# Router scores and ranks: from two TensorE products with the identity to a trip through memory, and the choice of kept tokens one step later

## What is computed

```python
scores = jnp.einsum('bld,d->bl', x, w_r) + b_r
_, idx = jax.lax.top_k(scores, k)
x_sel = jnp.take_along_axis(x, idx[:, :, None], axis=1)
h = jax.nn.gelu(jnp.einsum('bkd,df->bkf', x_sel, w1) + b1)
out_sel = jnp.einsum('bkf,fd->bkd', h, w2) + b2
out = jnp.zeros_like(x).at[batch_ix, idx].set(out_sel)
```

## Time and profile before

| | |
|---|---|
| median of 3 runs | 1942.69 us (1942.07 to 1943.33) |
| profiled execution, its own time | 1942.34 us |
| its span, first to last instruction | 1940.5 us |
| mean granted TensorE clock | 0.986 |
| PE, DVE, ACT, POOL busy | 95%, 75%, 65%, 65% of the span |
| router's first and last product with the identity | start at 1005.4 us and 1857.8 us |

### The profile page before, as it was taken

One profiled execution on the slowest core, in us unless ns is written; L12 is line 12 of the kernel. 1 busy time (PEld: TensorE's weight loads), 2 busy tenths in 40 slices (PEclk: granted clock), 3 DMA queues, 4 the chain that ended last, 5 costly groups with the idle time before them and its releaser, 6 DMA issues.

```text
span 1940.5 us, 30226 instructions
## 1 busy us (share of the span) xinstructions
PE 1837.5 (95%) x9439; PEld 1281.6 (66%) x9439; DVE 1456.8 (75%) x2572; ACT 1260.5 (65%) x3937; POOL 1265.2 (65%) x1252
## 2 busy tenths in 40 slices
PE   6889999999999999988599899999999999999998
PEld 6667777777777777655255575756657575665765
DVE  8889999999999999997555565655656565565522
ACT  5778888888888888865355574655646465564621
POOL 4779999999999999988676545444544544450000
PEclk9999999999999999999699999999999999999999
DMA  5333223332333323320767334434343343431021
GB/s 203 128 127 143 110 112 138 144 132 100 127 144 144 133 95 132 131 87 29 209 203 206 112 89 111 120 108 122 93 139 99 109 119 108 119 94 59 29 66 39
DMA packets 133198, 228.59 MB, mean 118 GB/s; under 512 B 31076, under 2 KB 86388, under 8 KB 128048
## 3 DMA queue, kind: packets, MB, share of 16 engines
q1 hardware_dynamic: 99952, 161.38, 23.9%
q0 software_dynamic: 33088, 65.28, 12.0%
HBM read 209.99 MB, written 44.70 MB: 131 GB/s over the span
## 4 chain that ended last, share of the span: by engine, by line
PE 46%; ACT 2%; issue 1%; DMA 1%; DVE 1%; POOL 0%; DVEq 0%; SPq 0%; ACTq 0%; POOLq 0%
PE attn_psum L1909 12%; PE attn_psum L1925 11%; PE attn_psum L1828 5%; PE attn_psum L1841 5%; PE attn_psum L1821 4%; PE attn_psum L1867 3%; PE attn_psum L1812 2%; PE attn_psum L1943 2%; PE attn_psum L1802 1%; PE attn_psum L1853 1%; ACT xh L1554 1%; ACT th L1555 1%; DMA kv_at<-kv_scratch,new_now 0%; ACT prob L1512 0%; ACT k_t L1502 0%
## 5 line engine op out<-in xcount | busy, mean ns | idle before, releaser
L996 DVE TENSOR_TENSOR_SCAN hid<-scan_psum,dbu 128x1024 f32<-128x1024 f32 x256 | 593.8, 2320 | 10.6 <-ACT scan_psum L635 10.6
L1161 PE MATMUL scan_psum<-hid,ident 128*128 128x256 f32 x2048 | 519.0, 384 | 24.1 <-POOL hid L492 23.8
L1161 PEld LDWEIGHTS scan_psum<-hid,ident 128*128 128x128 f32 x2048 | 378.8, 191 | 185.7 <-issue 106.5
L1663 DVE CUSTOM_DVE_ANT_0 prob<-attn_psum,mask 128x336 f32<-128x336 f32 x256 | 120.1, 505 | 287.2 <-PE attn_psum L1821 287.0
L492 POOL TENSOR_TENSOR hid<-hid,kv_at 128x1024 f32<-128x1024 f32 x128 | 306.5, 2407 | 29.8 <-DVE hid L996 29.4
L492 POOL TENSOR_TENSOR hid<-hid,bc 128x1024 f32<-128x1024 f32 x128 | 305.8, 2401 | 28.6 <-DVE hid L996 28.2
L1518 ACT COPY p_t<-attn_psum 112x384 f32<-112x384 f32 x256 | 122.3, 484 | 291.5 <-PE attn_psum L1828 291.5
L1925 PE MATMUL attn_psum<-w,ffn_hid 128*128 128x512 f32 x512 | 239.0, 596 | 4.9 <-DVE y_sb L1728 4.9
L1446 POOL DMA_INDIRECT kv_at<-kv_scratch,new_now x189 | 200.4, 1060 | 61.6 <-issue 57.0
L1909 PE MATMUL attn_psum<-xs_in,w 128*128 128x256 f32 x1024 | 232.6, 381 | 7.5 <-ACT xs_in L1524 6.6
L635 ACT ACTIVATE scan_psum<-delta,neg_a 128x252 f32<-128x252 f32 x512 | 211.3, 464 | 10.6 <-DVE hid L996 10.6
(11 more groups left out here) (222 smaller groups left out, 3047.7 us busy)
## 6 DMA issues: line engine op xcount, KB each, us to landing
bc<-bc_scratch SPq DMA_DIRECT2D x16, 2048.0 KB, 7.4
kv_at<-bc_scratch SPq DMA_DIRECT2D x15, 2048.0 KB, 7.3
q_scratch<-qg SPq DMA_DIRECT2D x32, 260.0 KB, 2.0
early<-q_scratch SPq DMA_DIRECT2D x32, 260.0 KB, 3.0
x_pair<-in_x_pairs SPq DMA_DIRECT2D x32, 256.0 KB, 2.7
kv_scratch<-kvg SPq DMA_DIRECT2D x32, 256.0 KB, 2.0
a_scratch<-a_sb SPq DMA_DIRECT2D x32, 256.0 KB, 3.2
w_o<-x_scratch SPq DMA_DIRECT2D x32, 256.0 KB, 3.2
```

The lines of the kernel that those rows point to most:

```text
L996: nc.vector.tensor_tensor_scan(hid[:, k % RING, :, :].rearrange("p n t -> p (n t)"), decay[k % 2], dbu[:, k % RING, :, :].rearrange("p n t ...
L1161: mm = nc.tensor.matmul(yc, ident[:], hid[:, k % RING, i, :], start=False, stop=(k % 4 == 3 and i == 3))
```

## The change

The two products with the identity are gone. `r_s` is stored to a scratch row in memory (`store_scores`) and loaded back as the whole row on every partition (`load_scores`, into `s_row`); `r_rank` goes the same way into 64 partitions of `rank_row`. VectorE compares with `r_s` itself, so the product that gave `r_own` goes too. `router_keep` moves from window 1 to window 2. `turn_o` waits for the copy of the previous output out of the bank instead of for the previous selection. In pairs 31 to 33 some of the work sits at other windows, since windows 2 and 3 are short or empty there. The fill of `ones` and TensorE's wait for it go.

```diff
@@ SyncE
+            def store_scores(m):
+                sp.wait_ge(dve_s, m + 1)
+                sp.dma_start(S["score"][m], r_s[:]).then_inc(st_s, 16)
+            def load_scores(m):
+                sp.wait_ge(st_s, 16 * (m + 1))
+                wait(sp, dve_rank, m)
+                sp.dma_start(s_row[:], S["score"][m:m + 1].rearrange("m p o -> (m p o)").partition_broadcast(P)
+                             ).then_inc(ld_s, 16)
+            def store_ranks(m):
+                sp.wait_ge(dve_rank, m + 1)
+                sp.dma_start(S["rank"][m], r_rank[:]).then_inc(st_rank, 16)
+            def load_ranks(m):
+                rows = slice(64 * (m % 2), 64 * (m % 2) + 64)
+                sp.wait_ge(st_rank, 16 * (m + 1))
+                wait(sp, dve_keep, 2 * m)
+                sp.dma_start(rank_row[rows, :], S["rank"][m:m + 1].rearrange("m p o -> (m p o)").partition_broadcast(64)
+                             ).then_inc(ld_rank, 16)
...
                 if parts.prev2:
+                    store_ranks(m - 2)
+                    load_ranks(m - 2)
                     store_keep(m - 2, 2 * i + j // 2 - 1, h)
...
+                if parts.prev:
+                    store_scores(m - 1)
                 if parts.second and j in (1, 2):
                     store_out(i - 2, j - 1)
+                if parts.prev:
+                    load_scores(m - 1)
@@ GpSimd
-            nc.gpsimd.memset(ones[:], 1.0).then_inc(filled, 1)
@@ ScalarE
-                    if w == 2 and parts.prev:
+                    if w == (2 if parts.own else 1) and parts.prev:
                         take_a(m - 1, 2 * i + j // 2, 1 - h)
@@ VectorE
             def router_rank(m):
-                row = a_bank[:, 0:P]
-                dve.wait_ge(pe_row, m + 1)
-                v.tensor_tensor_reduce(r_junk[:, 0:P], row, ident[:], 1.0, 0.0, ALU.mult, ALU.add, r_own[:]
-                                       ).then_inc(dve_rc, 1)
-                dve.wait_ge(dve_rc, 4 * m + 2)
-                v.scalar_tensor_tensor(r_junk[:, P:2 * P], row, r_own[:], own[:], ALU.is_gt, ALU.mult,
+                dve.wait_ge(ld_s, 16 * (m + 1))
+                dve.wait_ge(dve_s, m + 1)
+                v.scalar_tensor_tensor(r_junk[:, P:2 * P], s_row[:], r_s[:], own[:], ALU.is_gt, ALU.mult,
                                        accum_out=r_gt[:]).then_inc(dve_rc, 1)
...
             def router_keep(m, i, j):
-                dve.wait_ge(pe_rank, m + 1)
+                dve.wait_ge(ld_rank, 16 * (m + 1))
...
-                        if w == 3:
+                        if w == (3 if parts.own else 1):
                             router_score(m - 1)
                     if parts.prev2:
                         if w == 0:
                             router_rank(m - 2)
-                        if w == 1:
+                        if w == (2 if parts.nxt else 1):
                             router_keep(m - 2, i if j > 1 else i - 1, (j - 2) % 4)
@@ TensorE
             def turn_o(m):
                 pe.wait_ge(act_o, m + 1)
-                wait(pe, dve_keep, 2 * m)
+                wait(pe, act_a, m)
...
-            def router_row(m):
-                pe.wait_ge(act_a, m + 1)
-                pe.wait_ge(dve_s, m + 1)
-                nc.tensor.transpose(a_bank[:, 0:P], r_s[:].to_broadcast([P, P]), ident[:]).then_inc(pe_row, 1)
-            def router_ranks(m):
-                pe.wait_ge(dve_rank, m + 1)
-                nc.tensor.transpose(a_bank[:, P:2 * P], r_rank[:].to_broadcast([P, P]), ident[:]).then_inc(pe_rank, 1)
...
-                    if w == 2 and parts.prev:
+                    if w == (2 if parts.own else 1) and parts.prev:
                         turn_o(m - 1)
...
-            pe.wait_ge(filled, 1)
```

More of the change, by code:

```diff
@@ L1205, in attention_ffn_block @@
         ident = W["ident"]
-        ones = sb("ones", [P, P])
         w_o = sb("w_o", [P, 4, D])
@@ L1240, in attention_ffn_block @@
         r_idx = [sb(f"r_idx{i}", [P, 1], I32) for i in range(2)]
-        r_own, r_gt, r_eq, r_rank = (sb(n, [P, 1]) for n in ("r_own", "r_gt", "r_eq", "r_rank"))
+        r_gt, r_eq, r_rank = (sb(n, [P, 1]) for n in ("r_gt", "r_eq", "r_rank"))
+        s_row, rank_row = sb("s_row", [P, P]), sb("rank_row", [P, P])
         keep_t = [sb(f"keep_t{i}", [P, P]) for i in range(2)]
@@ L1676, in router_score @@
                 dve.wait_ge(act_a, m + 1)
[L1677 removed]
+                wait(dve, st_s, 16 * m)
+                wait(dve, dve_rank, m)
                 v.tensor_tensor_reduce(r_junk[:], a_sb[:], w_or[:], 1.0, 0.0, ALU.mult, ALU.add, r_s[:]
                                        ).then_inc(dve_rc, 1)
[L1680 removed]
+                dve.wait_ge(dve_rc, 3 * m + 1)
                 v.tensor_tensor(r_s[:], r_s[:], b_r[:], ALU.add).then_inc(dve_s, 1)
             def router_rank(m):
[L1685 to L1690 removed]
+                dve.wait_ge(ld_s, 16 * (m + 1))
+                dve.wait_ge(dve_s, m + 1)
+                v.scalar_tensor_tensor(r_junk[:, P:2 * P], s_row[:], r_s[:], own[:], ALU.is_gt, ALU.mult,
                                        accum_out=r_gt[:]).then_inc(dve_rc, 1)
[L1692 removed]
+                v.scalar_tensor_tensor(r_junk[:, 2 * P:3 * P], s_row[:], r_s[:], before[:], ALU.is_equal, ALU.mult,
                                        accum_out=r_eq[:]).then_inc(dve_rc, 1)
[L1694 removed]
+                dve.wait_ge(dve_rc, 3 * m + 3)
+                wait(dve, st_rank, 16 * m)
                 v.tensor_tensor(r_rank[:], r_gt[:], r_eq[:], ALU.add).then_inc(dve_rank, 1)
@@ L1700, in router_keep @@
                 rows = slice(64 * h, 64 * h + 64)
-                dve.wait_ge(pe_rank, m + 1)
+                dve.wait_ge(ld_rank, 16 * (m + 1))
                 wait(dve, st_keep[h], 16 * (2 * i + j // 2))
-                v.scalar_tensor_tensor(keep_t[h][rows, :], a_bank[rows, P:2 * P], slot_no[rows, :], slot_own[rows, :],
+                v.scalar_tensor_tensor(keep_t[h][rows, :], rank_row[rows, :], slot_no[rows, :], slot_own[rows, :],
                                        ALU.is_equal, ALU.mult).then_inc(dve_keep, 1)
@@ L1957, in pair @@
                         turn_x(i - 1, j - 1)
-                    if w == 0 and parts.prev2:
-                        router_row(m - 2)
-                    if w == 1 and parts.prev2:
-                        router_ranks(m - 2)
                     if w < 2 and parts.own:
@@ L2010, in program @@
     S["wid"] = nc.dram_tensor("wid_scratch", [NWC, P], F32).ap()
+    S["score"] = nc.dram_tensor("score_scratch", [NG, P, 1], F32).ap()
+    S["rank"] = nc.dram_tensor("rank_scratch", [NG, P, 1], F32).ap()
     S["keep"] = nc.dram_tensor("keep_scratch", [NG, 2 * SEL, P], F32).ap()
```

9 lines of the change are left out of this document (3 added, 6 removed).

## The result

The changed kernel takes 2062.05 us (median of 6 runs, 2055.58 to 2069.25), the kernel before 1942.38 (6 runs, 1941.41 to 1943.33): 1.0617 of it, 95% interval 1.0594 to 1.0639. The forecast was 1939.4 us, with a chance of 0.12 for slower. The profiled execution has a span of 2059.7 us, 119.2 more than before.

The account below looks back on a forecast made before the run. TensorE was taken to bound the second phase; 3.9 us saved on products less 0.6 us lost in pairs 2 to 4 gave -3.3 us, so 1939.0 on the profiled execution and 1939.4 as median, range 1935.5 to 1945.

Parts of the forecast that it names:

- The scores' trip, steady: Pairs 7 to 30: store and load back take 5.4 us, inside a gap of 5.8 to 7.7; cost 0.
- the sign of its being wrong: The prediction is wrong if a round trip through memory takes over 9 us; one of three such signs.
- The rival on the other side: Scores' trip slow in every pair, 4-byte pieces being slower; at 10 us a trip 1958 us; chance 0.12, above 1946.6.
- The cover, 9.2 us: Steady pairs: 5.8 us gap plus 3.4 us slack; a scores' trip costs TensorE time only above 9.2 us.
- What leaves TensorE, 6.8 us: 64 products, two for each of 32 pairs, at 0.106 us each: at most 6.8 us saved.
- what is absorbed: 27 of 64 removed products stand ahead of TensorE stops and buy nothing; 37 remain, 3.9 us saved, bounds 3.5 and 6.8.
- the three stops: TensorE's waits for `xs_in`, `y_sb` and at `turn_k`, on average 0.8, 0.7 and 0.36 us, grow by 0.1 each.
- Pairs 2 to 4, 0.6 us (0 to 4): Ranks' store queues behind weight loads, VectorE stands 8 us at `router_keep`, `norms` barely on time; 0.6 us lost, bounds 0 and 4.
- The tail, 0 us (at most 2): Last pairs: the last gather lands at 1867 or 1868.6, ahead of TensorE's need at 1870.82; cost 0, upper bound 2 us.
- The ranks' trip, 0: Steady pairs: the ranks' trip has a whole window more, 13 us or so; cost 0.
- VectorE's added work: L1687 goes, about 0.3 us a pair, and compares read SBUF; VectorE is not the bound, so 0.
- the start: Removing the fill of `ones` at 948.97 saves 0 to 0.2 us; taken as 0.

Follow-up runs that it names:

- x9: Repeat of the changed kernel with scores and ranks turned by VectorE's 32x32 transpose, stored as four pieces of 128 bytes: 1936.71 us, 0.9975 of the kernel before.
- x1: The changed kernel, but VectorE turns scores and ranks first, so each store is four pieces of 128 bytes: 1937.33 us, 0.9976 of the kernel before.
- x2: The kernel before with the changed kernel's four transfers a pair added and read by nobody; rows and ranks still come by products: 1944.4 us, 1.0013.
- x10: The changed kernel with the scores' 4-byte store kept, the ranks' store turned and the compare in window 1: 1962.57 us, 1.0104 of the kernel before.
- x13: The changed kernel with turned stores and three added scores' stores, each waited for, in a disturbed time: 1.0205 of the kernel before.
- x17: Turned stores with three added scores' stores again, in another disturbed call: 1.0263 of the kernel before.
- x12: The changed kernel with turned stores and the scores stored twice, one after the other has landed: 1936.35 us, 0.9971 of the kernel before.
- x4: The kernel before with only the ranks sent through memory and tokens chosen in window 2; scores by the product: 1950.93 us, 1.0043.

## Why the prediction was wrong, step by step

**The step that failed** is in "The scores' trip, steady": "The nearest are the store of `keep_t`, 2.1 us to landing ... 2.1 + 3.2 + 0.1 = 5.4 us, just inside." The store took 7.2 us and the load 4.2 to 4.9, so the trip was 11.4 us in the pair shown and 12.7 in the median. That is above the 9 us that the prediction itself named as the sign of its being wrong. The row of `keep_t` was taken as nearest, but it has pieces of 512 bytes and the new store pieces of 4; with four pieces of 128 bytes the step is right (1.55 us). The Trainium skill (DMA: Bandwidth & Descriptors, Anatomy of one DMA), which the prediction quoted, puts the fixed cost at about 2.0 us, for transfers that GpSimd issues. The trace of x9 has 1.55 us for the turned store, near it; the changed kernel's has 7.3 for the column, far from it. The same page of the Trainium skill (Specifications) says that below 512 bytes the DMA engine reads, modifies and writes. The prediction did not weigh that. It would fit a slow column, but it doesn't explain it by itself, since the pieces of 128 bytes are below 512 too and were quick.

**The rival on the other side was the right one**, "128 pieces of 4 bytes are slower than the 512-byte rows", at 0.12. x1 and x9 show that this store makes the loss, x2 and x10 that in the steady part its traffic costs nothing and the wait does; x13 and x17 lose time with a wait of VectorE and no 4-byte store, if in a disturbed time. What made 1958 out of it was "at 10 us" and its silence on the two ends and on the clock. Its formula comes near the steady loss: 12.7 - 9.2 = 3.5 us in 3 of 4 pairs is 52.5 us over 20 pairs, measured 50.6. But that is luck, as its 9.2 and its pairs show.

**The cover, 9.2 us, was read wrongly.** It adds the gap of one kind of pair (5.8 us) to the slack of another (3.4 us). The slack of 3.4 us stands behind a gap of 6.6, and the gap of 5.8 has 4.7 us of slack behind it. These rows of the kernel before, where `r_s` is ready at 1243.03 (the end of the first) and the scaled `prob` at 1278.81 (the end of the third), complete the two:

```profile
1242.87 0.16 DVE L1681 TENSOR_TENSOR r_s<-r_s,b_r 128x1 f32<-128x1 f32 x1
...
1249.63 0.29 DVE L1687 CUSTOM_DVE_ANT_0 r_junk<-attn_psum,ident 128x128 f32<-128x128 f32 x1
...
1278.41 0.40 DVE L1670 TENSOR_SCALAR prob<-prob,share 128x336 f32<-128x336 f32 x1
...
1283.46 0.49 PE L1828 MATMUL attn_psum<-ident,prob 128*112 128x128 f32 x3
```

So the cover is 6.6 + 3.4 = 10.0 us for the scores of pair 9 (compared in pair 11) and of every fourth pair after it, 5.8 + 4.7 = 10.5 for those of pair 10, and by the same reading 14.8 and 14.6 for those of pairs 11 and 12, and so on in turn. Nor do 3 of 4 pairs have the tight gap: 5.8 us is that of one in four. The loss lies accordingly: between pairs 8 and 28 the four kinds lose 28.4, 14.5, -0.5 and 8.2 us. By these covers the trips are too long by 30.2 us in sum. The other 20 us are not in that sum; TensorE's longer busy time, 13.8 us, is beside them, but what links the two was not tested. x12, whose trips from `r_s` to the compare take 6.7 to 10.0 us in these pairs, never goes beyond its covers and loses nothing. No undisturbed trip between that and the changed kernel's was measured.

**What leaves TensorE, 6.8 us, and what is absorbed.** Right, once the trips are short: x9 gains 0.13 us a pair in the steady part, 4.7 by its span, 5.3 by the medians; forecast 3.9, bounds 3.5 and 6.8. Of the three stops two grew as said, by 0.11 us each time: `y_sb` from 4.9 to 5.7 us in 7 stops, `k_t` from 4.7 to 6.1 in 13. The stop for `xs_in` stayed at 6.6 in 8. So 20 products were absorbed, not 27: 6.8 - 20 x 0.106 = 4.7. Why that copy came earlier was not looked into.

**Pairs 2 to 4, 0.6 us (0 to 4).** The changed kernel lost 32.1 us from pair 1 to 6. With turned stores VectorE waits 5.8 and 5.3 us for `rank_row` in pairs 2 and 3 (forecast 4 to 8), and TensorE nothing: the place was read rightly, its price hung on the same store. Alone, the ranks' small store costs 5.1 us there (x4), and the scores' 12.3 even with the compare in window 1 (x10).

**The tail, 0 us (at most 2).** It cost 34.7 us. It has four small stores in a row of dependent steps, each 5 to 6 us longer than a turned one, and the clock falls in the gaps; x9 lost 0.2. The place was named ("if SyncE's queue or VectorE's residual behind `router_keep` runs later than that"), the size rested on the same store.

**The ranks' trip, 0.** Right in the steady part (x4), wrong at both ends.

**VectorE's added work and the start, 0.** Nothing in x9 contradicts it: two added turns a pair lie in VectorE's idle time.

**The clock** was no term at all: I took 1.00 throughout. Longer busy time at the lower clock is a third of the loss.

With 12.7 us for the trip the prediction's own working gives 1939.4 + 24 x 3.5 = 2023 us, the right sign and two thirds of the loss, by the lucky formula; what it leaves out are the two ends and the clock.

## What to carry to other kernels

Price a transfer by its pieces, not by its bytes alone: a column of one value a partition, stored packed, is the slowest of the eight shapes tried here (7.3 us), and turning it with VectorE's 32x32 transpose (0.2 us) makes it 1.6. A wait put into an engine that isn't the bound is free only up to its slack, and every instruction behind it in that engine's row shares the wait; place what waits where a whole window lies between, and count start and end of the pipeline apart, because they have no spare window. Add gap and slack of the same pair, not of two. Mark the pairs and subtract: totals of x10 alone would have led to the wrong cause.
